# Preparation of a graph-network kernel: transfers of 125 partitions in two parts, statistics in three batches, first loads of the score stage issued in the preparation

## The reference, cut to what matters

```
xn  = layernorm(x)                                   # eps 1e-5
h   = (xn * rsqrt(mean(xn**2) + 1e-6) * rms_w) @ W_down          # 1250 x 256
xl  = h @ Wl ; xr = h @ Wr                                       # 4 heads of 64
e   = sum(leaky_relu(xl[src] + xr[dst], 0.2) * att)              # edges and self loops
gnn = (softmax of e over the edges of each dst, times xl[src], summed by dst) @ W_up
k,v,q = xn @ Wk + bk, xn @ Wv + bv, xn @ Wq + bq                 # 16 heads of 64
mix = (phi(q) @ (phi(k)^T v per head)) @ Wo + bo                 # phi = elu + 1
x1  = x + gnn + mix
out = x1 + nvfp4_ffn(layernorm(x1))                              # 1024 -> 512 -> 1024, fake-quantised
```

## Time and profile before

| | us |
|---|---|
| median of 3 runs | 1208.81 |
| lowest, highest | 1203.96, 1210.78 |
| the profiled execution, its own time | 1211.81 |
| its span in the trace | 1210.0 |
| PE busy | 988.6 (82%) |
| DVE busy | 907.4 (75%) |
| ACT busy | 597.4 (49%) |
| POOL busy | 386.8 (32%) |

### The profile page before, as it was taken

The page is one execution under the profiler, slowest core; times in us unless marked ns, Lnnn a source line. Parts: engine busy times, 40 slices in busy tenths (PEclk is TensorE's granted clock), DMA queues, the critical chain, the costliest instruction groups (busy, mean ns, idle before and its releaser), DMA issues. The chain is left out here.

```text
span 1210.0 us, 16332 instructions
## 1 busy us (share of the span) xinstructions
PE 988.6 (82%) x5021; PEld 800.6 (66%) x5021; DVE 907.4 (75%) x1499; ACT 597.4 (49%) x1346; POOL 386.8 (32%) x383
## 2 busy tenths in 40 slices
PE   0586889999999999999523788888888999999933
PEld 0574789999999999999512577667673344444412
DVE  3796568878788688778863799999952478887893
ACT  0243556675666666656404487786661124332421
POOL 0212777777777677777002000000001000000000
PEclk9899889999999999999855899999897999999966
DMA  4301888988889788888589776666560313332222
GB/s 158 109 17 35 249 257 259 272 262 262 264 266 295 229 274 261 258 267 248 180 164 249 230 249 224 238 212 217 161 217 3 98 55 97 100 75 68 51 34 34
DMA packets 104079, 217.81 MB, mean 180 GB/s; under 512 B 21668, under 2 KB 54013, under 8 KB 103887
## 3 DMA queue, kind: packets, MB, share of 16 engines
q1 hardware_dynamic: 83951, 161.41, 39.8%
q0 software_dynamic: 18464, 53.79, 19.8%
q10 hardware_dynamic: 1584, 1.57, 0.4%
HBM read 156.83 MB, written 70.45 MB: 188 GB/s over the span
## 5 line engine op out<-in xcount | busy, mean ns | idle before, releaser
L872 POOL DMA_INDIRECT score_gath<-xl_rows,misc x324 | 343.2, 1059 | 114.6 <-issue 95.1
L1484 PE MATMUL agg_ps_o<-agg_gath,agg_hot 128*125 128x256 f32 x648 | 190.4, 430 | 39.7 <-DVE agg_hot L1589 39.3
L912 PE MATMUL score_ps_m<-x_hi,score_w_hi 128*128 128x416 f32 (+1 forms) x576 | 209.5, 364 | 2.7 <-DVE score_w_lo L1065 2.7
L913 PE MATMUL score_ps_m<-x_lo,score_w_hi 128*128 128x416 f32 (+1 forms) x576 | 204.5, 355 | 0.0
L914 PE MATMUL score_ps_m<-x_hi,score_w_lo 128*128 128x416 f32 (+1 forms) x576 | 204.0, 354 | 0.0
L1535 ACT ACTIVATE agg_gath<-agg_gath,prob 128x64 f32<-128x64 f32 x648 | 159.2, 337 | 26.4 <-DMA agg_gath<-edge_rows 26.4
L1046 DVE TENSOR_TENSOR score_zb<-score_gath,score_ps_x 128x1024 f32<-128x1024 f32 x81 | 98.8, 1219 | 70.6 <-PE score_ps_x L895 68.2
L1795 PE MATMUL fin_ps_y<-mix_w,phi_c 128*125 128x512 f32 x320 | 143.9, 603 | 3.7 <-DVEq L1905 2.8
L1484 PEld LDWEIGHTS agg_ps_o<-agg_gath,agg_hot 128*125 128x125 f32 x648 | 100.6, 194 | 63.1 <-issue 54.9
L1486 PE MATMUL agg_ps_o<-ext,agg_hot 128*125 128x18 f32 x324 | 120.0, 370 | 0.0
L1795 PEld LDWEIGHTS fin_ps_y<-mix_w,phi_c 128*125 128x125 f32 x320 | 61.0, 191 | 80.8 <-issue 75.5
(11 more groups left out here) (314 smaller groups left out, 1586.9 us busy)
## 6 DMA issues: line engine op xcount, KB each, us to landing
edge_rows<-score_gath SPq DMA_DIRECT2D x81, 520.0 KB, 4.0
agg_gath<-edge_rows SPq DMA_DIRECT2D x81, 520.0 KB, 3.7
score_local_bc<-local_rows SPq DMA_DIRECT2D x40, 250.0 KB
score_gath<-xl_rows,misc POOLq DMA_INDIRECT x324, 5.1
x_rows<-in_x SPq DMA_DIRECT2D x10, 500.0 KB
xb_rows<-in_x SPq DMA_DIRECT2D x1, 5000.0 KB, 18.0
xb_rows<-in_L_mix_bo POOLq DMA_DIRECT2D x1, 5000.0 KB, 36.6
phi_c<-phi_rows SPq DMA_DIRECT2D x10, 500.0 KB, 3.8
```

What stands on the lines that cost most here:

```text
L872: nc.gpsimd.indirect_dma_start(out=gath[:, g % GS, q, :], out_offset=None, in_=xl_rows, in_offset=bass.IndirectOffsetOnAxis(ap=src_idx[:, ...
L912: pe.matmul(acc, w_hi[:, i % 2, kk, :], x_hi[:, kk, cols], start=(kk == 0), stop=False)
L913: pe.matmul(acc, w_hi[:, i % 2, kk, :], x_lo[:, kk, cols], start=False, stop=False)
L1484: pe.matmul(o_flat[0:C, ds(cs[q] * HID, HID)], lhs.bitcast(F32), gath[:, g % GS, q, 0:HID], start=False, stop=False, skip_group_check=True)
```

## The change

Five edits, all but the last part of the first in the preparation:

1. Transfers between DRAM and tiles of 125 partitions that the diff touches (x, dst, `next_i`, the stores of `xl_rows`, and `local_bc` in all of the score stage) are issued as two DMAs, of partitions 0 to 111 and 112 to 124. `src_i` stays whole.
2. Chunk 0 of x is loaded ahead of dst, and ACT waits for chunk 2 before it issues the loads of `wd` and `wlr`.
3. The statistics are made in batches of chunks 0 and 1, 2 to 4, and 5 to 9. The first batch's bn_stats stand ahead of the edge check, the border counts behind the second root of the first batch; low parts 0 and 1 go around the second batch's bn_stats.
4. The scaling of W_down stands ahead of the numbers that set the gather lists (`bounds`, `tile_i`), and PE takes the transposes of chunks 0 and 1 ahead of the columns and counts.
5. `w_raw` and `local_bc` lie in the memory of `x_rows`, slots 0 to 2, and the first two loads of each are issued by SP in the preparation, once all chunks are transposed, ahead of the stores of `xl_rows`.

```diff
+ROWS_SPLIT = slice(0, 112), slice(112, C)
+def local_load(sp, k, b):
+    groups = min(LB, NG - LB * b)
+    flat = k.local_rows.rearrange("(a r) t -> a (r t)", a=1)
+    for part in ROWS_SPLIT:
+        sp.dma_start(k.local_bc[part, b % 2, 0:groups, :]..., flat[...].to_broadcast(...)).then_inc(k.s_loc[b % 2], 16)
+def weight_load(sp, a, k, i):
+    sp.dma_start(k.w_raw[:, i % 2, :, :], ...).then_inc(k.s_raw[i % 2], 16)
-        XB, HB = 7, 5
+        XB, BATCHES = 7, [(0, 2), (2, 5), (5, NC)]
@@ sync, prepare
+                load_x(0)                                   # two DMAs: ROWS_SPLIT
+                for part in ROWS_SPLIT: sp.dma_start(o.dst_i[part, :], ...)
+                for part in (slice(0, 112), slice(112, C - 1)): sp.dma_start(o.next_i[part, :], ...)
...
                 for c in range(XB, NC):
                     sp.wait_ge(s_tr, c - XB + 1)
-                    sp.dma_start(x_rows[:, c % XB, :], a["x"][C * c:C * c + C, :]).then_inc(s_x[c], 16)
+                    load_x(c)
...
+                sp.wait_ge(s_crow, 48)
+                sp.wait_ge(s_tr, NC)
+                for b in range(2):
+                    local_load(sp, k, b)
+                    weight_load(sp, a, k, b)
                 for c in range(NC):
                     sp.wait_ge(s_rowx, c + 1)
-                    sp.dma_start(xl_rows[C * c:C * c + C, :], xl_keep[:, c, :]).then_inc(s_store[c % 2], 16)
+                    for part in ROWS_SPLIT:
+                        sp.dma_start(xl_rows[C * c:C * c + C, :][part, :], xl_keep[part, c, :]).then_inc(s_store[c % 2], 16)
@@ tensor
                 for i in range(NC + 4):
...
+                    if i == 1:
+                        columns_and_counts()
@@ scalar
+                act.wait_ge(s_x[2], 32)
                 act.dma_start(wd[:, :, :], ...)
...
+                root(0, 0)
+                root(0, 1)
+                copy_xt(0)
+                root(1, 0)
+                copy_xt(1)
+                root(1, 1)
+                high_down()
+                for i in range(2, NC + 4):                  # root(2, 0), root(2, 1) ahead of i == 4
@@ vector
+                moments(0)
+                (edge check: dst_f, next_i, is_lt, reduce)
+                layer_scale(0)
+                (flag, branch)
+                normalise(0)
+                normalise(1)
+                rms_scale(0)
+                (nine counts)
+                low_part(0)
+                moments(1)
+                low_part(1)
+                layer_scale(1)
+                for c in range(2, 5):
+                    normalise(c)
+                rms_scale(1)
+                (rms_col, bias, eight scalings of wd; then bounds ... tile_i, chunk, att)
+                low_part(2)
                 v.wait_ge(s_wdh, 1)
                 v.tensor_tensor(wd_lo[:, :, :], wd[:, :, :], wd_hi[:, :, :].bitcast(F32), ALU.subtract).then_inc(s_wdl, 1)
-                low_part(1)
-                low_part(2)
                 low_part(3)
-                statistics(1)
+                moments(2)
+                layer_scale(2)
+                normalise(5)
+                normalise(6)
+                rms_scale(2)
@@ score, sync
-                local(0)
-                load_weights(0)
-                local(1)
-                load_weights(1)
                 load_tile(0)
@@ score, scalar
-                    act.wait_ge(s_loc[g // LB % 2], 16 * (g // LB // 2 + 1))
+                    act.wait_ge(s_loc[g // LB % 2], 32 * (g // LB // 2 + 1))
```

More of the change, by code:

```diff
@@ L35 @@
 SLOTS = 5
+LB = 2
+ROWS_SPLIT = slice(0, 112), slice(112, C)
 PERJ = 10
@@ L91, in allocate @@
     k.s_rows = ctx.enter_context(nc.semaphore("s_rows"))
+    k.s_loc = [ctx.enter_context(nc.semaphore(f"s_loc{i}")) for i in range(2)]
+    k.s_raw = [ctx.enter_context(nc.semaphore(f"s_raw{i}")) for i in range(2)]
     k.s_gath = [ctx.enter_context(nc.semaphore(f"s_gath{i}")) for i in range(SLOTS)]
@@ L147, in allocate_last @@
     k.x_bo = ctx.enter_context(nc.sbuf_tensor("x_bo", [C, 2, D], F32))
+PANEL_ITEMS = [(j, role) for j in range(PANELS) for role in range(3)]
+PANEL_NAMES = "L0_mix_Wk", "L0_mix_Wv", "L0_mix_Wq"
+def local_load(sp, k, b):
+    groups = min(LB, NG - LB * b)
+    flat = k.local_rows.rearrange("(a r) t -> a (r t)", a=1)
+    for part in ROWS_SPLIT:
+        sp.dma_start(k.local_bc[part, b % 2, 0:groups, :].rearrange("p g t -> p (g t)"),
+                     flat[:, LB * b * GP * TE:(LB * b + groups) * GP * TE].to_broadcast([part.stop - part.start, groups * GP * TE])
+                     ).then_inc(k.s_loc[b % 2], 16)
+def weight_load(sp, a, k, i):
+    j, role = PANEL_ITEMS[i]
+    sp.dma_start(k.w_raw[:, i % 2, :, :], a[PANEL_NAMES[role]].rearrange("(k p) o -> p k o", p=P)[:, :, j * P:(j + 1) * P]
+                 ).then_inc(k.s_raw[i % 2], 16)
 def prepare(nc, a, k):
@@ L478, in _, with root @@
                 act.dma_start(wlr[:, :, HID:], a["L0_gnn_Wr"].rearrange("(k p) n -> p k n", p=P)).then_inc(s_w, 16)
[L480 to L487, removed]
+                def root(n, i):
+                    cs = slice(*BATCHES[n])
+                    act.wait_ge(s_sq, 2 * n + i + 1)
+                    act.activation(sm[:, 2 * i + 1, cs], sm[:, 2 * i, cs], ACT.Sqrt).then_inc(s_root, 1)
                 def copy_xt(c):
@@ L530, in _, with moments @@
             def _(v):
-                q = Steps(v, s_ov)
-                v.wait_ge(s_dsti, 64)
-                q.mark(v.tensor_copy(o.dst_f[:, :], o.dst_i[:, :]))
-                q.do(v.tensor_copy(scratch[:, :], o.next_i[:, :]))
-                q.do(v.tensor_tensor(scratch[:, :], scratch[:, :], o.dst_f[:, :], ALU.is_lt))
+                oq = Steps(v, s_ov)
+                q = Steps(v, s_v)
+                def moments(n):
+                    first, end = BATCHES[n]
+                    for c in range(first, end):
+                        v.wait_ge(s_x[c], 32)
+                        for h in range(2):
+                            q.mark(v.bn_stats(stats[:, c, h, :], x_rows[:, c % XB, h * 512:(h + 1) * 512]))
+                    q.wait()
+                    for c in range(first, end):
+                        q.mark(v.bn_aggr(mean_var[:, c, :], stats[:, c, :, :].rearrange("p a b -> p (a b)")))
+                    q.wait()
+                    q.do(v.tensor_scalar(sm[:, 0, first:end], mean_var[:, first:end, 1], 1e-5, None, ALU.add))
+                    v.sem_inc(s_sq, 1)
@@ L782, in score @@
         s_kept = [sem(f"s_kept{i}") for i in range(GS)]
-        s_loc = [sem(f"s_loc{i}") for i in range(2)]
+        s_loc, s_raw = k.s_loc, k.s_raw
         s_mt = sem("s_mt")
@@ L789, in score @@
         s_sc = sem("s_sc")
-        s_raw = [sem(f"s_raw{i}") for i in range(2)]
         s_whi = sem("s_whi")
```

192 lines of the change are left out of this document (92 added, 100 removed).

## The result

The changed kernel takes 1204.97 us (median of 20 runs, 1202.49 to 1208.24), the kernel before 1211.05 us beside it on the same chip: ratio 0.9956, 95% interval 0.994 to 0.9972. The profiled execution took 1203.13 us with a span of 1201.2 us (before 1211.81 and 1210.0). The forecast was 1202.7, or 0.5% less; measured is 0.44% less. In us the medians of 20 runs are 6.1 apart, and 6.1 was forecast. The size came out, but not for the reasons given, as the stages show. Stages are read from one profiled execution of each kernel.

The account below looks back on a forecast made before the run. PE was taken to bound the score stage (busy 416 of 425 us), while the early preparation waits. Preparation -4.3, stores -0.3 as summed, head start 0, `local_bc` -1.5 make -6.1 us: 1208.8 to 1202.7 us, range 1195.5 to 1209.

Parts of the forecast that it names:

- The start of the preparation, step by step: Preparation: chunks land sooner, first Sqrt at 11.1 us, `wd_lo` ends at 44.1, low part 3 comes 4.3 us earlier (1.8 to 6.7).
- rival B: Preparation gains little, from third batch, late table load, low parts' waits or late x: -2.1 us, 1206.7 us; chance 0.22.
- the 1.2 us of a colder PE: Preparation, before low part 3: PE, idle some ten microseconds, runs matmuls and transposes at low clock, 0.7 to 1.6 us more.
- `local_bc` in two parts all through the stage: Score stage: ACT's 103.1 us of waits are covered; only PE's stalls and lost clock can be won, -1.5 us (0 to -5).
- the five of sixteen engines: Transfers of 125 partitions: about five of sixteen DMA engines work; in two parts a chunk takes 1.6 us instead of 4.09.
- Head start: Score stage start: early first loads start PE about 5.3 us sooner, lost at the third panel's weights; value 0 (+0.5 to -1.5).
- Store end: Split stores of `xl_rows`: the last store ends about half a microsecond behind DVE, 0.3 us more taken (0 to 0.5).
- Rival A: Score stage keeps PE's head start, 5.3 us more go: -11.4 us, 1197.4 us; chance 0.15.
- rival C: Score stage slower: each of SP's 39 extra issues costs 0.33 us at the weights and PE, +8.3 us, 1217.1 us; chance 0.06.
- three signs of being wrong: Low part 3 under 1.8 or over 6.7 us earlier; PE's long wait not longer; stage from 165 us changing over 5 us.

Follow-up runs that it names:

- roots first: Changed kernel with ACT's wait for chunk 2 and its three weight loads moved behind the first batch's two roots: 1199.57 us, 0.9911 to the kernel before.
- the other kernel with this preparation: Changed kernel with ACT's wait and weight loads behind the first batch's roots and `local_bc` as one DMA of 128 partitions: 1201.46 us, 0.9919.
- the doubled load: Kernel before, with each `local_bc` load in the score stage followed by the same 125 rows sent to a spare DRAM tensor: 1228.73 us, 1.0134.
- the late loads: Changed kernel with the first two loads of `local_bc` and of the weights issued back in the score block: 1203.03 us, 0.9939.
- the split alone: Kernel before with only `local_bc` loaded in parts of 112 and 13 partitions in the score stage: 1202.38 us, 0.9929.
- the transfers to 128 partitions: `local_bc` as one 128-partition DMA: on the kernel before with x in two parts, 0.986; on the changed kernel with weight loads behind the roots, 0.9919.
- the later runs: Beside the kernel before at 1295.9 us: changed without ACT's chunk 2 wait, 1.0004; before with x split and `local_bc` on 128, 0.9935; that plus dst split, 0.9934.
- the best version: Kernel before with x in parts of 112 and 13 and `local_bc` as one 128-partition DMA: 1192.28 us, 0.986; run again later 1286.61 us, 0.9935.

## Why the prediction was right in size and wrong in its parts

| us | forecast | changed | roots first |
|---|---|---|---|
| chunks 0, 1, 2 landed | 4.5, 6.5, 8 | 5.3, 9.2, 11.1 | 5.1, 8.5, - |
| first square root | 11.1 | 18.05 | 10.35 |
| `wd_lo` ends | 44.1 | 50.6 | 44.4 |
| DVE's wait for low part 3 | 6.8 | 6.90 | 7.22 |
| first gather | 115.0 | 119.94 | 114.19 |

**The step that failed is in "The start of the preparation, step by step": "ACT waits for chunk 2, issues three DMAs (2.41 - 0.80 = 1.6) and loads its table".** Two numbers in it were wrong, and both push the same root. Chunk 2 came 3.1 us late: 0.8 us with chunk 0, 1.9 between chunks 0 and 1, where I had allowed 2.0 us for a chunk and dst's rows and 3.9 were taken, and 0.45 between chunks 1 and 2. I had priced transfers at the 325 GB/s of the earlier trace rows; sixteen engines moved 240 to 281 here. And the three issues took 5.6 us (16.75 - 11.12) instead of 1.6: I had taken a price from the start of the kernel for issues behind the loads of x. The third of them took 0.51 us before and 4.49 us here; what holds it is not shown. Together 7.1 us, which is the lateness of the root (6.95) and of `wd_lo` (6.5). The preparation gave +0.3 instead of -4.3 us: worse than rival B, whose cause (late x, late table load) is the one found. With the issues moved, the steps from the first root on hold within 0.9 us, though chunk 1 is 2.0 us late there too, and the preparation gains 5.5 us (3.3 us in the other kernel with this preparation, whose first gather came at 116.32).

One term of the preparation was put in for nothing, the 1.2 us of a colder PE. By the sum DVE would wait 6.8 + 1.2 = 8.0 us for low part 3; it waited 6.90, and 7.22 with the roots first. PE had been idle for 9.98 us, and its matmuls still ran at the pace of before: 18 in 3.71 us from 50.6 to 54.6 us, against 19 in 3.73 us from 49.6 to 53.6 before. The granted clock is 1.00 (2.4 GHz) in the first of these windows and 0.56 (between the two levels) in the second, so here it does not tell the pace.

The Trainium skill, "ScalarE: Activation LUTs", section "What ACT_TABLE_LOAD costs", puts a drain of about 1.4 us on top of the load. Here the load starts 0.02 us behind the last issue and the root 0.02 us behind the load's 1.28 (16.75 to 18.05): no drain shows. Nor does one where ACT was busy just before: in the final stage of the changed kernel a root ends at 993.83 us, a load starts at 993.85, ends at 995.13, and the next activation starts at 995.15.

**"`local_bc` in two parts all through the stage" was mis-sized**: -1.5 us, bound -5, against -7.1 alone and about -8 in the change. The step that failed is "PE is busy nearly throughout, so that time was covered": of ACT's 103.1 us nearly all was covered, but the 6.0 us of PE's own waits were not, and each counted for more than its length (4.1 us for 2.3 us of standing). The two terms of my bound, 5 us of idle time and 1% of clock (4.2 of 425 us), make 9, not the 5 that I wrote; the gain lies inside 9. Nor did I ask whether the loaded engines also carry gathers and weights, which the doubled load shows (+14.7 us).

PE's busy time in the 425 us is the same before and after (416.07, 415.46), because that window runs past the stage's end, which comes sooner now. One that ends within the stage shows the gain, before and after:

```profile
165.00:575.00 410.00, 403.92 (x2433) 397.72 (x2433) 329.62 (x376) 262.26 (x404) 306.43 (x289) 0.99 0.87 263
```

```profile
165.00:575.00 410.00, 406.83 (x2468) 401.94 (x2467) 333.10 (x381) 266.19 (x412) 306.78 (x290) 1.00 0.87 267
```

On the five of sixteen engines, the share of 0.32 in the earlier trace rows had pointed to them, and taking load off them (0.9929) and loading them twice (1.0134) move the time in opposite directions. By the rule of the Trainium skill, "DMA: Bandwidth & Descriptors", "Why a DMA increments its semaphore by 16 and not by 1" (the largest number up to 16 that divides the partitions), 125 gives 5 and 112 gives 16. The runs agree: a share of 0.32 with 125 partitions, 1.03 and 1.05 with 112 and 13 (6 to 10 us).

**Head start: right in value, wrong in course.** PE had it at the first group and not from the fifth on. I had put the loss at the seventh, with a wait of about 9.8 us behind the weights, but the third `local_bc` took it already: PE waited 3.91 us at the fifth group and 1.25 at the seventh. **Store end:** the last store's wait fell from 2.4 to 1.1 us, too little for the times to show. **Rival A** (head start kept) is refuted by the late loads, **rival C** (the 39 issues) by the split alone and by the transfers to 128 partitions. The prediction named three signs of being wrong, and all three came: low part 3 came 1.1 us later (57.53 against 56.41), PE's long wait shrank instead of lengthening (4.54 to 1.25 us), and the stage from 165 us on gained 6 us (-2.0 at the seventh group, -8.0 at the 80th) where at most 5 were allowed. The total was right by luck: two errors of 4.6 and 6.5 us had opposite signs.

## What to carry to other kernels

Give transfers a partition count that sixteen divides: broadcast to 128 where the target allows it, else split (112 and 13), and do so first for those that run beside everything else. A weight load issued by ACT is an instruction of ACT: behind other transfers it can hold ACT for microseconds (4.49 here), so nothing that others wait for may stand behind it. And price late transfers by the waits of the bound engine that go back to them, each at one and a half to two times its length, not by the waits of the engines beside it.

## What the runs showed that was not expected

With a share of 1.03 to 1.06 the engines moved 240 to 281 GB/s here and 325 before; at 0.32 they moved 129, so five moved about half of what sixteen did, not a third. The same DMA issue of ACT took 0.51 us at the start of the kernel and 4.49 us behind the loads of x (SP had one of 5.86 us with x alone split). The same preparation ended at 114.19 and 116.32 us in two kernels. In the later runs the kernel before was 7% slower and the best version 8%, with PE idle nearly six times as long.
